# Products of constants in TensorE's waits, and a joined head in the third attention

## What is computed

```
q = rope(query @ Wq)        # 32 heads of 128
k = rope(key @ Wk)          # 8 heads of 128, each used by 4 query heads
v = value @ Wv
scores = q @ k.T / sqrt(128), -1e9 where mask == 0
out = softmax(scores) @ v  @ Wo
cos, sin = rope tables at position_ids (512 positions)
```

## Time and profile before

| | us |
|---|---|
| median of 3 runs | 1829.8 (1827.31 to 1829.89) |
| the profiled execution | 1831.94, its span 1830.6 |
| PE busy | 1634.0 (89% of the span) |
| DVE / POOL / ACT busy | 1023.6 / 578.8 / 501.7 |
| mean granted TensorE clock | 0.942 of full speed |

### The profile page before, as it was taken

One profiled execution on the slowest core, in us unless ns is written; L12 is line 12 of the kernel. 1 busy time (PEld: TensorE's weight loads), 2 busy tenths in 40 slices (PEclk: granted clock), 3 DMA queues, 4 the chain that ended last, 5 costly groups with the idle time before them and its releaser, 6 DMA issues.

```text
span 1830.6 us, 21084 instructions
## 1 busy us (share of the span) xinstructions
PE 1634.0 (89%) x8794; PEld 1170.7 (64%) x8794; DVE 1023.6 (56%) x1327; ACT 501.7 (27%) x743; POOL 578.8 (32%) x370
## 2 busy tenths in 40 slices
PE   8879989998799589999899999989789877779998
PEld 3254358886388457777677777768645445547886
DVE  6987852224624625554554555555552388576666
ACT  4220020103322123233232324322101477640000
POOL 4826732220543213132231313221031144461221
PEclk9979989999999798999999999999889999899999
DMA  2000041002000120101010110100300012400000
GB/s 117 1 1 1 0 162 46 24 0 121 12 0 1 58 92 24 35 24 35 24 58 9 50 35 23 35 1 1 140 0 15 8 25 48 163 15 6 13 12 18
DMA packets 18015, 66.47 MB, mean 36 GB/s; under 512 B 1440, under 2 KB 9760, under 8 KB 13312
## 3 DMA queue, kind: packets, MB, share of 16 engines
q1 hardware_dynamic: 17920, 65.12, 10.3%
HBM read 58.82 MB, written 2.10 MB: 33 GB/s over the span
## 4 chain that ended last, share of the span: by engine, by line
PE 68%; DVE 17%; POOL 7%; ACT 4%; issue 3%; DMA 1%; SPq 0%; DVEq 0%; ACTq 0%; POOLq 0%
PE banks L270 41%; PE banks L264 21%; POOL arena L1521 3%; DVE arena L1365 2%; PE banks L392 2%; DVE arena L435 1%; PE banks L1810 1%; DVE arena L234 1%; POOL w_lo L2273 1%; POOL arena L1526 1%; POOL grouped_split L1540 1%; ACT arena L1455 1%; ACT arena L1454 1%; PE banks L2072 1%; PE banks L277 1%
## 5 line engine op out<-in xcount | busy, mean ns | idle before, releaser
L270 PE MATMUL banks<-grouped_split 128*128 128x512 f32 x1536 | 390.7, 409 | 11.7 <-DVE grouped_split L1393 8.3
L270 PEld LDWEIGHTS banks<-grouped_split 128*128 128x128 f32 x1536 | 292.1, 195 | 78.8 <-DVE grouped_split L1393 9.4
L1521 POOL TENSOR_TENSOR arena<-arena,grouped 128x512 f32<-128x512 f32 x80 | 104.9, 1316 | 402.2 <-ACT arena L1455 402.2
L270 PE MATMUL banks<-experts_split 128*128 128x512 f32 (+1 forms) x792 | 181.7, 392 | 1.9 <-DVE experts_split L620 1.9
L270 PEld LDWEIGHTS banks<-experts_split 128*128 128x128 f32 (+1 forms) x792 | 146.6, 185 | 36.3 <-issue 2.4
L1361 DVE TENSOR_TENSOR arena<-banks,grouped 128x512 f32<-128x512 f32 x80 | 54.6, 683 | 169.7 <-ACT arena L1455 169.7
L1365 DVE TENSOR_TENSOR arena<-arena 128x512 f32<-128x512 f32 x80 | 88.4, 1106 | 64.4 <-POOL arena L1521 63.6
L264 PEld LDWEIGHTS banks<-arena 128*128 128x128 f32 x624 | 95.0, 216 | 27.3 <-issue 19.8
L264 PE MATMUL banks<-arena 128*128 128x64 f32 (+1 forms) x624 | 104.7, 321 | 7.3 <-DMA arena<-in_c 6.6
L648 DVE SCALAR_TENSOR_TENSOR arena<-banks,experts,arena 128x512 f32<-128x512 f32 x64 | 47.8, 751 | 111.3 <-PE banks L270 111.3
L264 PE MATMUL banks<-dense 128*32 128x64 f32 (+4 forms) x1738 | 87.7, 303 | 23.2 <-ACT dense L1918 9.2
(11 more groups left out here) (282 smaller groups left out, 3015.3 us busy)
## 6 DMA issues: line engine op xcount, KB each, us to landing
grouped<-in_attn SPq DMA_DIRECT2D x16, 1024.0 KB, 5.1
experts<-in_expert SPq DMA_DIRECT2D x8, 1024.0 KB, 4.9
linear<-in_ffn SPq DMA_DIRECT2D x1, 4096.0 KB, 14.9
grouped<-in_attn SPq DMA_DIRECT2D x8, 512.0 KB, 3.7
dense<-arena SPq DMA_DIRECT2D x16, 256.0 KB, 4.9
dense<-in_w SPq DMA_DIRECT2D x1, 3584.0 KB, 13.8
dense<-in_attn SPq DMA_DIRECT2D x1, 3072.0 KB, 12.5
dense<-in_w SPq DMA_DIRECT2D x1, 2688.0 KB, 10.1
```

Of the source, the lines that this page charges most:

```text
L270: s = pe.matmul(dst, lhsT=lhsT[i], rhs=rhs[j], start=(k == 0 and x == 0), stop=(k == n - 1 and x == 2))
L1521: g_.tensor_tensor(rot, rot, f(SIN + h * HALF, HALF), ALU.mult).then_inc(rot_sin.sem, 1)
```

## The change

It adds `stay_busy`, n plain f32 products of 256 columns of constants into a bank that nobody reads, at four places: 22 in `attn0` before the wait for `low_done(4)`, 16 before the start of `attn2` (behind a wait for the last read of bank 7 by `ffn1`), six in every `apply(g, 0)` between the value products of k = 0 and k = 1, and 15 before the start of `ffn2`. Each of them multiplies the identity with the identity and the first columns of a 0/1 selector.

The head of `attn2` is joined with its first rows: the loads go positions, k and v weights, q weights, tables (to a place of their own), mask, output weights, with no wait between them; DVE splits the q weights and the tables before it makes the one-hot tiles, and prepares the mask last; PE makes both k rows and two q rows, then the table products, now fp32r with the high and the low part of the tables against the exact one-hot tiles (32 instructions of 512 columns), then the two other q rows. ACT makes the high parts of the q weights and of the tables before it copies cosines and sines out.

```diff
+def stay_busy(m, pe, b, n):
+    for _ in range(n):
+        mm(pe, m.bank[:, b, 0:256], m.const("ident"), m.A[:, CONST:CONST + 256])
 ...
 (attn0, tensor, behind the sum products)
+        stay_busy(m, pe, 7, 22)
         pe.wait_ge(*selt_done(1))
         pe.wait_ge(*low_done(4))
 ...
 (ffn1)
+    m.rows_read = lat_out(NT)
 (attn2, sync)
         sp.wait_ge(*start)
-        m.load(sp, STG_KV, dram["rope"], rope_in)
         sp.dma_start(f(POS, N).bitcast(I32), dram["pos"]).then_inc(pos_in.sem, 16)
+        group_load(sp, 0, 2048, 3072, STG_KV, kv_in)
+        group_load(sp, 0, 0, 2048, STG_Q, q_in)
+        m.load(sp, STG_ROPE, dram["rope"], rope_in)
         sp.dma_start(f(MK, N).bitcast(I32), dram["mask"]).then_inc(mask_in.sem, 16)
-        group_load(sp, 0, 0, 2048, STG_Q, q_in)
-        sp.wait_ge(*rope_mm(4))
-        group_load(sp, 0, 2048, 3072, STG_KV, kv_in)
         group_load(sp, 0, 3072, 5120, STG_O, o_in)
 ...
 (attn2, tensor)
+        pe.wait_ge(*m.rows_read)
+        stay_busy(m, pe, 7, 16)
         pe.wait_ge(*start)
 ...
-        pe.wait_ge(*pos_set(4))
-        pe.wait_ge(*rope_in(16))
-        (the 16 table products of L1202 to L1207)
-        pe.wait_ge(*rope_out(4))
         pe.wait_ge(*xlo(NT))
 ...
                 pe.wait_ge(*turn_out(2 * (2 * g + h) + k + 1))
+                if (h, k) == (0, 1):
+                    stay_busy(m, pe, 7, 6)
                 pair = [take(("a", g, h, 2 * k + b2)) for b2 in range(2)]
 ...
+        def positions():
+            pe.wait_ge(*rope_lo(1))
+            for c in range(MAXPOS // P):
+                pe.wait_ge(*pos_set(c + 1))
+                for j in range(2):
+                    for h in range(2):
+                        for x in range(2):
+                            s = pe.matmul(bank[:, 4 + 2 * j + h, :], lhsT=ropes[x][:, c * 2 * D2 + j * D2:][:, 0:D2],
+                                          rhs=hot[:, c * N + h * HALF:c * N + (h + 1) * HALF], start=c + x == 0,
+                                          stop=(c == MAXPOS // P - 1 and x == 1))
+                        if c == MAXPOS // P - 1:
+                            s.then_inc(rope_mm.sem, 1)
 ...
-        for q in range(QH2):
-            q_rows(0, q, 0)
+        q_rows(0, 0, 0)
+        q_rows(0, 1, 0)
+        positions()
+        q_rows(0, 2, 0)
+        q_rows(0, 3, 0)
 (attn2, vector, behind the low parts of x)
-        (mask, then positions)
+        v.wait_ge(*wq_hi(1))
+        v.tensor_tensor(wqs[1], f(STG_Q, LQ), wqs[0].bitcast(F32), ALU.subtract).then_inc(wq_lo0.sem, 1)
+        v.wait_ge(*rope_hi(1))
+        v.tensor_tensor(ropes[1][:, :], f(STG_ROPE, 1024), ropes[0][:, :].bitcast(F32), ALU.subtract).then_inc(rope_lo.sem, 1)
+        (positions with the one-hot tiles as fp32r, then mask)
         v.wait_ge(*rope_out(4))
-        v.wait_ge(*wq_hi(1))
-        v.tensor_tensor(wqs[1], f(STG_Q, LQ), wqs[0].bitcast(F32), ALU.subtract).then_inc(wq_lo0.sem, 1)
 ...
 (attn2, scalar, behind the high parts of x)
+        act.wait_ge(*q_in(16))
+        act.activation(wqs[0], f(STG_Q, LQ), ACT.Copy).then_inc(wq_hi.sem, 1)
+        act.wait_ge(*rope_in(16))
+        act.activation(ropes[0][:, :], f(STG_ROPE, 1024), ACT.Copy).then_inc(rope_hi.sem, 1)
         (the four copies of L1444)
-        act.wait_ge(*q_in(16))
-        act.activation(wqs[0], f(STG_Q, LQ), ACT.Copy).then_inc(wq_hi.sem, 1)
 ...
 (ffn2, tensor)
+        stay_busy(m, pe, 6, 15)
         pe.wait_ge(*start)
```

More of the change, by code:

```diff
@@ L1138, in attn2 @@
     ROT, QC = C, C + 1024
+    STG_ROPE = STG_KV + 1024
     SPLIT = R + 13312
@@ L1161, in attn2 @@
     start = m.end
+    hot = m.buf("attn2_hot", XT, 4 * N, F32R)
+    ropes = [m.buf(f"attn2_rope_{n}", C + 2048 + 1024 * i, 1024, F32R) for i, n in enumerate(("hi", "lo"))]
+    rope_hi, rope_lo = m.sem("attn2_rope_hi"), m.sem("attn2_rope_lo")
     xs = [r(XTS + x * DC * N, DC * N, DC, N) for x in (0, 1)]
@@ L1335, in vector @@
                             xs[0][:, :, t * P:(t + 1) * P].bitcast(F32), ALU.subtract).then_inc(xlo.sem, 1)
-        v.wait_ge(*mask_in(16))
+        v.wait_ge(*wq_hi(1))
+        v.tensor_tensor(wqs[1], f(STG_Q, LQ), wqs[0].bitcast(F32), ALU.subtract).then_inc(wq_lo0.sem, 1)
+        v.wait_ge(*rope_hi(1))
+        v.tensor_tensor(ropes[1][:, :], f(STG_ROPE, 1024), ropes[0][:, :].bitcast(F32), ALU.subtract).then_inc(rope_lo.sem, 1)
         v.wait_ge(*pos_in(16))
-        m.own(v, v.tensor_scalar(f(MNEG, N), f(MK, N).bitcast(I32), 0.0, None, ALU.is_equal))
-        m.own(v, v.tensor_scalar(f(MK, N), f(MNEG, N), -1.0, 1.0, ALU.mult, ALU.add))
-        v.tensor_scalar(f(MNEG, N), f(MNEG, N), NEG / scale2, None, ALU.mult)
         m.own(v, v.tensor_copy(f(POS, N), f(POS, N).bitcast(I32)))
@@ L1345, in vector @@
         for c in range(MAXPOS // P):
-            v.tensor_scalar(f(XT + c * N, N), f(POS, N), m.const("posid")[:, c:c + 1], None,
+            v.tensor_scalar(hot[:, c * N:(c + 1) * N], f(POS, N), m.const("posid")[:, c:c + 1], None,
                             ALU.is_equal).then_inc(pos_set.sem, 1)
+        v.wait_ge(*mask_in(16))
+        m.own(v, v.tensor_scalar(f(MNEG, N), f(MK, N).bitcast(I32), 0.0, None, ALU.is_equal))
+        m.own(v, v.tensor_scalar(f(MK, N), f(MNEG, N), -1.0, 1.0, ALU.mult, ALU.add))
+        v.tensor_scalar(f(MNEG, N), f(MNEG, N), NEG / scale2, None, ALU.mult)
         v.wait_ge(*rope_out(4))
-        v.wait_ge(*wq_hi(1))
-        v.tensor_tensor(wqs[1], f(STG_Q, LQ), wqs[0].bitcast(F32), ALU.subtract).then_inc(wq_lo0.sem, 1)
         def rotary(u):
```

## The result

The changed kernel takes 1806.37 us (median of 4 runs, 1804.94 to 1808.94), the kernel before on the same chip 1829.85: 23.5 us less, ratio 0.987 (95% interval 0.9847 to 0.9894). One later execution of the kernel before took 4027.56 us and is left out of the ratios of experiments 2 to 4.

The account below looks back on a forecast made before the run. PE, busy 89%, was taken as the bound, at half clock behind its waits. Groups -12.3, head -18.0, first attention -2.0, dense block -1.8 gave -34.1 us: 1796 us, range 1790 to 1802 (0.48), wider 1785 to 1808 (about 0.85).

Parts of the forecast that it names:

- The six products in the groups: Second value products of half 0: filling the wait keeps full clock, seven stretches of 8.21 us instead of 75.14 in all.
- the cover: Steady groups: the six products end 0.45 us before DVE releases the second value products, so they cost nothing there.
- the falls at half 1: Shorter waits of half 1: clock falls in four groups, two more than before, costing 3.2 us (-3.2 to +8.0).
- The last group: No k rows to wait for there, so the six are in the way: +1.9 us, from +0.9 to +3.5.
- The head: Start of `attn2`, joined with its first rows: first q rows with scores come 17.2 us sooner.
- the wait for the tables: Before the third q row, whose bank hangs on the tables: one new wait, from 649.9 to about 652.5.
- the rival of the rotation chain: Head: DVE's rotations, all started at 650, take 2 us each, not 1.4; head gains 12, 1802 us; chance 0.1.
- The scores behind the head: Scores after the head, mostly at half clock: another start gains up to 4 us or nothing, taken as 0.8.
- The dense block: Before `ffn2`: 15 products speed up PE's transposes so ACT sets the pace, -1.8 us, from 0 to -2.
- The first attention: `attn0`: 22 products in 11.52 us of idle time quicken the products behind them, -2.0 us, from 0 to -3.2.
- that constants don't count as work: Rival, all four places: the clock falls during the products of constants, 0.86 us each; 1844 us; chance 0.05.
- "falls move" rival: Groups: clock falls at half 1 in all, or sometimes behind second value products, +8 to +10 us, 1805; chance 0.22.

Follow-up runs that it names:

- experiments 2 to 4: Changed kernel without the last group's six products (1798.2 us); with three or twelve instead of six (1806.8, 1817.3); with two more in half 1's wait (1797.1).
- e1: The changed kernel without the six products in the groups; 1811.1 us, ratio 0.9872.
- e2: The kernel before with nothing but the six products in each group; 1817.4 us, ratio 0.9916.
- e3: The kernel before with the joined head alone, no product of constants anywhere; 1808.7 us, ratio 0.9875.
- e5: The changed kernel with the six products left out in the last group only; 1798.2 us, ratio 0.9815.
- e6: The changed kernel with three products instead of six in each group; 1806.8 us in its one run.
- e8: The changed kernel with two more products in the wait of half 1, in each group but the last; 1797.1 us, ratio 0.9795.
- e11: Changed kernel without the last group's six, with two in half 1's wait, two before the centroid products, 26 instead of 22 in the first attention; 1791.3 us.
- e9: The changed kernel with twelve products instead of six in each group; 1817.3 us in its one run.

## Why the prediction was right, and where it wasn't

The time, 1806.4, lies in the range of 1785 to 1808, near its upper end, but above the 1790 to 1802 that I had given the greatest weight; the direction was right; the forecast of 34.1 us was 10.6 too much against the medians, 7.7 in the trace. Of the 7.7, 4.3 are the dense block and 2.9 the scores behind the head.

- **The six products in the groups**: right in mechanism and size. The stretches go to 8.40 us in the steady groups (forecast 8.21), the cover is 0.24 us (0.45), and the falls at half 1 are four, as I had taken. The four were a pick between none and seven, and luck: the other kernels with six products and nothing in the wait of half 1 had two to four. -13.9 against -14.5 us; e1 and e2 show the same 11 to 14 us by themselves.
- **The last group**: +3.0 against +1.9, within its bounds. The term was mis-sized since the constants ran in part at half clock (4.12 us).
- **The head**: -16.7 against -17.2, with its steps: k rows 7.9 us after the start of the transposes (8.3), the wait for the tables 2.81 (2.6), the two q rows 8.56 (6.8, a fall). The sum came right by two errors that cancel. PE was ready for the third q row 1.3 us sooner than forecast, but from there to the scores it took 11.90 us, forecast 10.1. That is the rival of the rotation chain, in part: I had taken the last wait as 3.35 us, as before, and it is so only because the q rows ran partly at half clock. In e3 they ran at full clock, 6.08 us, and the wait grew to 5.28; from the third q row to the scores it is 11.4 us in all seven kernels where DVE's chain of rotations alone sets that time, and 11.9 in the four where the q rows end later. DVE's additions (L1384 of e3) come 1.85 us apart, where I had 1.4 and the rival 2. The chain starts from the tables, so they are still on the path.

```profile
652.48 6.08 PE L270 MATMUL banks<-grouped_split 128*128 128x512 f32 x24 [2.81 <-DVE arena L1380]
663.85 1.65 PE L270 MATMUL banks<-grouped_split 128*128 128x512 f32 x3 [5.28 <-DVE arena L1384]
```

- **The scores behind the head**: this is the step that failed. "Another start gains up to 4 us there or nothing, I take 0.8", and it lost. A fall of 13.66 us reached over the scores into the next q rows and PE came late to group 0. There the second value products now start 3.85 us after the first instead of 3.01, 0.84 more, and against DVE's row they are 1.7 late; I had 0.3. In all +2.4 instead of -0.5. The row was there: before, the same scores met a fall of 10.2 us, and nothing in it said that another start could only gain. In the eleven kernels with the joined head the fall there was 6.8, 10.2, 13.7 or 17.1 us long. What sets its length no run shows.
- **The dense block**: the other one. The 1.8 us of the transposes came (2.3 in the changed kernel; in all, e1, e5, e6 and e8 take 16.5 us against 17.6 to 19.0 without the 15), but I had priced what follows at nothing. In the changed kernel the clock fell 1.93 us into the centroid products, 64 columns each, and they took 12.19 us, +2.5 in all instead of -1.8. Whether the idle 1.04 us ahead of them made the clock fall isn't shown.
- **The first attention**: -2.5 in this pair of traces, -2.0 forecast, but right by chance: the experiments give some 1 us, and the fall that I wanted gone is there in every kernel.
- **The rivals**: that constants don't count as work is refuted by the 11 us at 1.00 in e11. The "falls move" rival had part of the truth, and its 1805 is the nearest to what came; but the falls at half 1, four instead of two, were already in the sum, and what came on top lay in the scores of group 0 and in the centroid products.

On the transposes, where the Trainium skill (TensorE: Matmul & The Clock Gate, Part 4) says that they don't count as activity, the windows of e3, which has no constants ahead of them, agree with the earlier trace rows and not with the page, and the traces decide: PE does nothing but transposes from 621.41 on, and the clock goes from 0.50 to 1.00 during them.

```profile
621.41:627.36 5.95, 5.80 (x26) 5.43 (x27) 5.84 (x12) 3.17 (x6) 0.80 (x1) 0.50 0.99 386
627.36:628.18 0.82, 0.82 (x7) 0.58 (x6) 0.66 (x2) 0.81 (x2) 0.00 (x0) 1.00 1.03 420
```

## What to carry to other kernels

Where PE waits for a fixed chain of other engines and is the bound again behind it, products that nobody reads can fill the wait and keep the clock up. Here six, which left a quarter of a microsecond, gave 1.8 us a group (e1); half the filling (e6) bought nothing, double (e9) cost 1.6 us a group. Put none where the next work is already waiting, and read what comes behind: in the changed kernel the thin centroid products, once at half clock, stayed there to their end. Judge such a change by matched marks in the trace, since the totals of one kernel lie up to 15 us apart, more than any one part gives but the head.

## What the runs showed that was not expected

- The kernel before ranges from 1827.3 to 1842.5 us on one chip, with a mean granted clock of 0.948 in its shortest run there and 0.938 in its longest. In the traces the falls in blocks that nobody touched lie elsewhere in each kernel.
- At half clock, products of 64 columns kept PE busy for 10.26 us without the clock rising. In eleven of the thirteen kernels the same products ran at 1.00 to their end (7.36 us); in the changed kernel and in e9 the clock fell 1.9 and 2.5 us into them.
- Three products in a wait of 3 us left longer times at half clock (10.2 us in three groups of seven) than none did in e1 (3.4 or 6.8 us).
